# Two more destination blocks summed from gathered rows in a two-layer graph convolution with experts

## What is computed

```python
x = x + gnn(layernorm(x), edges)        # two graph convolutions, each followed by relu
x = x + ffn(layernorm(x))               # top 2 of 8 experts, hidden size 1024, exact gelu

def gcn_conv(x, W, b, src, dst, n):
    h = x @ W
    src_sl, dst_sl = concat(src, arange(n)), concat(dst, arange(n))      # self-loops
    deg = segment_sum(ones_like(dst_sl), dst_sl)
    dinv = rsqrt(deg)
    msgs = h[src_sl] * (dinv[src_sl] * dinv[dst_sl])[:, None]
    return segment_sum(msgs, dst_sl) + b
```

## Time and profile before

| | us |
|---|---|
| runs, three | 2028.27, 2027.53, 2028.29 |
| median | 2028.27 |
| the profiled execution, its own time | 2047.49 |
| its span | 2045.8 |

### The profile page before, as it was taken

The page is one execution under the profiler, slowest core; times in us unless marked ns, Lnnn a source line. Parts: engine busy times, 40 slices in busy tenths (PEclk is TensorE's granted clock), DMA queues, the critical chain, the costliest instruction groups (busy, mean ns, idle before and its releaser), DMA issues. The chain is left out here.

```text
span 2045.8 us, 40624 instructions
## 1 busy us (share of the span) xinstructions
PE 1867.4 (91%) x13425; PEld 1222.5 (60%) x13426; DVE 1345.9 (66%) x3357; ACT 729.1 (36%) x1669; POOL 1146.3 (56%) x1208
## 2 busy tenths in 40 slices
PE   3679999999999998999999999935999999999997
PEld 2545555455555553544444444414989989989996
DVE  6585676676676662566676767567666676666664
ACT  3664444444444440111111111112444444444442
POOL 6215666566676644667666766302566565555553
PEclk8899999999999999999999999965999999999998
DMA  8264455455555437778877887724233322233322
GB/s 282 75 221 167 170 174 188 167 175 191 178 175 175 172 142 269 250 268 269 268 251 266 293 296 255 283 89 179 43 48 50 52 49 45 49 49 48 50 45 27
DMA packets 126408, 329.39 MB, mean 161 GB/s; under 512 B 20736, under 2 KB 80000, under 8 KB 119360
## 3 DMA queue, kind: packets, MB, share of 16 engines
q0 software_dynamic: 59072, 142.05, 26.2%
q1 hardware_dynamic: 47376, 167.36, 22.9%
q10 hardware_dynamic: 19824, 18.23, 2.8%
HBM read 214.10 MB, written 113.45 MB: 160 GB/s over the span
## 5 line engine op out<-in xcount | busy, mean ns | idle before, releaser
L943 PE MATMUL mp_o<-rows,m_counts 128*128 128x512 f16 x1960 | 490.3, 381 | 8.5 <-ACT m_counts L1073 8.5
L585 POOL DMA_INDIRECT m_x_t<-rows_d,take_src x311 | 366.5, 1178 | 204.0 <-PE mp_x L956 155.6
L1889 PE MATMUL rp_o<-rows,adj_ring 128*128 128x512 f16 x1960 | 455.9, 380 | 8.9 <-issue 8.9
L1816 POOL DMA_INDIRECT r_took<-rows_d,take_src x311 | 324.2, 1043 | 178.9 <-PE rp_g L1905 106.2
L1073 ACT ACTIVATE m_counts<-mp 128x490 f16<-128x490 f32 (+4 forms) x544 | 292.1, 559 | 351.9 <-PE mp L972 284.8
L1889 PEld LDWEIGHTS rp_o<-rows,adj_ring 128*128 128x128 f16 x1960 | 191.9, 98 | 225.9 <-issue 11.2
L2447 PE MATMUL fp_h<-f_xt,w 128*128 128x256 f16 x2688 | 305.1, 274 | 0.3 <-issue 0.3
L2466 PE MATMUL fp_y<-w,f_hh 128*128 x2688 | 302.4, 273 | 0.0
L943 PEld LDWEIGHTS mp_o<-rows,m_counts 128*128 128x128 f16 x1960 | 182.8, 98 | 185.2 <-issue 11.6
L2447 PEld LDWEIGHTS fp_h<-f_xt,w 128*128 x2688 | 264.3, 98 | 31.6 <-issue 0.7
L2466 PEld LDWEIGHTS fp_y<-w,f_hh 128*128 128x128 f16 x2688 | 263.0, 98 | 30.4
(11 more groups left out here) (257 smaller groups left out, 1913.0 us busy)
## 6 DMA issues: line engine op xcount, KB each, us to landing
adj<-m_counts SPq DMA_DIRECT2D x40, 1568.0 KB
adj_ring<-adj SPq DMA_DIRECT2D x40, 800.0 KB
adj_ring<-adj SPq DMA_DIRECT2D x40, 768.0 KB
r_raw<-in_L_ffn_W_dram POOLq DMA_DIRECT2D x16, 1024.0 KB
w_parts<-r_parts POOLq DMA_DIRECT2D x8, 1024.0 KB
w<-w_parts SPq DMA_DIRECT2D x4, 2048.0 KB
rows<-in_x_dram SPq DMA_DIRECT2D x7, 896.0 KB, 8.5
rows_d<-rows SPq DMA_DIRECT2D x7, 896.0 KB, 4.7
```

The lines of the kernel that those rows point to most:

```text
L585: pool.indirect_dma_start(out=took[:, r, :], out_offset=None, in_=k.rows_d[0], in_offset=bass.IndirectOffsetOnAxis(ap=k.take_src[:, i:i + ...
L943: mm = nc.tensor.matmul(ps_o[q], counts[:, q, s, :], k.rows[0][:, s, :], start=i == 0, stop=i == BLOCKS - 1)
L1816: pool.indirect_dma_start(out=took[:, r, :], out_offset=None, in_=k.rows_d[1], in_offset=bass.IndirectOffsetOnAxis(ap=k.take_src[:, i:i + ...
L1889: mm = nc.tensor.matmul(ps_o[b % 2], adj[:, m % ADJ_RING, at:at + P], rows[:, s, :], start=s == 0, stop=s == BLOCKS - 1)
```

## The change

DENSE goes from 40 to 38, so TAKEN from 9 to 11 and the TAKES from 311 to 381, in both layers. The banks go from 512 to 487 (4864 destinations are 486.4 banks), and the last of them, which reaches into a taken block, is emptied for the dense block alone. TAKE_END goes from 505 to 480, as the steps of layer one become fewer. To make room, four tables of aims and the layer norm's means and variances move into memory that the count buffers use later, and one small integer tile of layer two into the gates' tile.

```diff
-DENSE = 40
+DENSE = 38
 TAKEN = BLOCKS - DENSE
...
-TAKE_FROM, TAKE_END = 40, 505
+TAKE_FROM, TAKE_END = 40, 480
 TAKE_AT = [TAKE_FROM + i * (TAKE_END - TAKE_FROM) // len(TAKES) for i in range(len(TAKES))]
-BANKS_D = DENSE * P // SPAN
-COLS_D = BANKS_D // P
+BANKS_D = -(-DENSE * P // SPAN)
+COLS_D = -(-BANKS_D // P)
...
-        mv = carve(BLOCKS * 2).bitcast(fp32).rearrange("p (b n) -> p b n", n=2)
...
-        base_i = sb("m_base_i", [P, COLS, BANK_ITEMS], i32)
-        aim = sb("m_aim", [P, COLS, BANK_ITEMS], fp32)
-        aim_end = sb("m_aim_end", [P, COLS, BANK_ITEMS], fp32)
-        aim_neg = sb("m_aim_neg", [P, COLS, BANK_ITEMS], fp32)
...
+        spare = spare[:, SPAN * COLS * COL_BLOCKS:]
+        mv = spare[:, 0:4 * BLOCKS].bitcast(fp32).rearrange("p (b n) -> p b n", n=2)
+        spare = spare[:, 4 * BLOCKS:]
+        base_i, aim, aim_end, aim_neg = (
+            spare[:, 2 * n * COLS * BANK_ITEMS:2 * (n + 1) * COLS * BANK_ITEMS].bitcast(dt).rearrange("p (c j) -> p c j", c=COLS)
+            for n, dt in enumerate((i32, fp32, fp32, fp32)))
...
         def dst_blocks(n):
 
-            return sorted({n * SPAN // P, (n * SPAN + SPAN - 1) // P})
+            return [b for b in sorted({n * SPAN // P, (n * SPAN + SPAN - 1) // P}) if b < DENSE]
...
-        val_i = sb("_val_i", [P, BLOCKS], i32)
...
+        val_i = dense[:].rearrange("p b e -> p (b e)")[:, 0:BLOCKS].bitcast(i32)
```

More of the change, by code:

```diff
@@ L540, in _ @@
         def _(pool):
-            nc.gpsimd.iota(base_i[:], pattern=[[SPAN * P, COLS], [STEP, BANK_ITEMS]], base=0, channel_multiplier=SPAN).then_inc(ids, 1)
+            nc.gpsimd.iota(base_i, pattern=[[SPAN * P, COLS], [STEP, BANK_ITEMS]], base=0, channel_multiplier=SPAN).then_inc(ids, 1)
             nc.gpsimd.iota(ints[:], pattern=[[1, P]], base=0, channel_multiplier=0).then_inc(io_done, 1)
@@ L626, in _ @@
             dve.wait_ge(ids, 1)
-            nc.vector.tensor_scalar(aim_neg[:], base_i[:], -1.0, 0.5, ALU.mult, ALU.add)
+            nc.vector.tensor_scalar(aim_neg, base_i, -1.0, 0.5, ALU.mult, ALU.add)
             nc.vector.memset(limit_neg[:], 0.5 - BLOCKS).then_inc(cells_ready, 1)
-            nc.vector.tensor_scalar(aim_end[:], base_i[:], float(STEP), None, ALU.add)
+            nc.vector.tensor_scalar(aim_end, base_i, float(STEP), None, ALU.add)
             nc.vector.memset(one_h[:], 1.0)
-            link(nc.vector.tensor_copy(aim[:], base_i[:]))
+            link(nc.vector.tensor_copy(aim, base_i))
             dve.wait_ge(heads_in, 16)
@@ L732, in _ @@
             link(nc.vector.tensor_tensor(long[:, 0:COLS * BANK_ITEMS].rearrange("p (c j) -> p c j", j=BANK_ITEMS),
-                                         rows_d[:, :, :, P], aim_end[:], ALU.is_lt))
+                                         rows_d[:, :, :, P], aim_end, ALU.is_lt))
             nc.vector.tensor_reduce(long_any[:], long[:], AX.X, ALU.max).then_inc(long_ready, 1)
@@ L2106, in _ @@
             nc.vector.tensor_scalar(k.pad_value[:], k.token_id[:, BLOCKS - 1:BLOCKS], float(P + 1), None, ALU.add)
-            link(nc.vector.tensor_single_scalar(val_i[:], k.token_id[:], TOP_VALUE - 1, ALU.bitwise_and))
-            link(nc.vector.tensor_scalar(k.value[:], val_i[:], 1.0, None, ALU.add))
+            link(nc.vector.tensor_single_scalar(val_i, k.token_id[:], TOP_VALUE - 1, ALU.bitwise_and))
+            link(nc.vector.tensor_scalar(k.value[:], val_i, 1.0, None, ALU.add))
             nc.vector.memset(eps2[:], EPS * EPS).then_inc(eps_set, 1)
```

## The result

The changed kernel takes 2063.11 us (median of four runs, 2061.41 to 2068.16) against 2028.28 for the kernel before on the same chip: a ratio of 1.0181 with an interval of 1.0163 to 1.0199. It is slower by 34.8 us; the forecast was 6.4 slower. The sign was right and the size was not.

What follows compares the result with a forecast made beforehand. TensorE was taken to set the pace, with GpSimd following within a tenth to a fifth. Layer one -7.4, layer two +13.4 and set-up +0.4 gave +6.4 us on 2028.3: 2034.7 us, range 2010 to 2056.

Steps and rivals of the forecast that it cites:

- pitch term: Layer two: TensorE gains 5.6 us, GpSimd's 1.343 us a gather loses 19 (9.5 in each sixty-slot stretch); +13.4 us.
- rival (d): Layer two: gathers land late behind seven weight stores and loads, up to 6 us each; +19, 2053 us; chance 0.12.
- TensorE's side, layer one: Layer one: 35 blocks take 592.8 us, a gain of 13.4 us if TensorE keeps the pace.
- GpSimd's side, layer one: Layer one: GpSimd needs all the time TensorE's pace allows; 6 us lost, leaving -7.4 us.
- 568 of 568: no margin: Layer one: gathers and self-loop additions need 568 us of GpSimd, and TensorE's 429 steps last 568 us.
- The lead that I charged (6 us): Layer one: one ring lead of about 7 us estimated lost to brief lateness at equal speed, 6 us.
- The rule of the Trainium skill: Layer one: two-input tensor_tensor doesn't hold up GpSimd's descriptor generation, so the full 13.4 us would be gained; the prediction disagreed.
- GpSimd's side, layer two: Layer two: sixty dense slots need 195.7 us of GpSimd against TensorE's 179.2; 9.5 us lost twice, +19.
- The 20 easy slots ... restore the lead: Layer two: between dense stretches GpSimd needs 49.6 of TensorE's 57.1 us and regains its lead.
- (a): Both layers: TensorE keeps the pace, with GpSimd's pitch at 1.25 to 1.27; -18.6, 2009.7 us; chance 0.22.
- (b): Layer two's dense groups at pitch 1.30, 3.5 us lost twice, layer one's gain whole: 2016.7 us; chance 0.12.
- (c): Both layers wait for GpSimd, 5% above mean pitches: layer one +6.6, layer two +34, 2069 us; chance 0.10.

Runs made afterwards that it cites:

- run 1: Changed kernel with every layer-two weight load after the first fetching four columns, stores whole: 2045.09 us, ratio 1.0095.
- run 9: Changed kernel with four-column weight loads after the first, and weight loads and stores issued by ScalarE instead of GpSimd: 2036.59 us, ratio 1.0047.
- run 14: Changed kernel with layer two's gathers after the first eight fetching 64 rows instead of 128, and four-column weight loads after the first: 2043.41 us, ratio 1.0092.
- run 11: Kernel before the change with every layer-two weight load after the first fetching four columns: 2018.19 us, ratio 0.9954.
- run 7: Changed kernel with four-column weight loads after the first and eleven ring slots in layer two instead of eight: 2040.77 us, ratio 1.0066.
- run 2: Changed kernel with layer two's whole weight loads and stores issued by ScalarE instead of GpSimd: 2063.16 us, ratio 1.0177.

## Why the prediction was wrong

Two steps failed, both in layer two. The pitch term ("-5.6 + 19") was too small, since the lead covered less than the 7 us charged and TensorE's own pace was taken as 519 us in place of 509.8. And landings behind the weight transfers, rival (d), stood at nothing in the sum. That GpSimd would set the pace there was right.

**TensorE's side, layer one: right.** 592.8 us was worked out for TensorE's own pace and 594.4 measured.

**GpSimd's side, layer one: right in kind.** "568 of 568: no margin" is the trace after: 5.5 us of slack in all. The lead that I charged (6 us) was lost only to 1.6. The rule of the Trainium skill in "SBUF — State Buffer", Who interferes with whom, priced this layer nearer (-13.4 against -11.9 measured). Its reason isn't borne out: a gather still takes 1.193 us in the mean and 0.942 at least. Of the 381, the 180 beside no one-hot table of VectorE (L821) last 0.950 us in the mean, and each of the 126 above 1.3 us stands beside an m_oh_cell instruction.

**GpSimd's side, layer two: the term that failed.** It stood at 19 us; against TensorE's own pace it measured 37.1 (546.9 with small loads, less 509.8). The mechanism was right: two dense stretches lose, the easy slots between them don't. The sizes were not. Layer two can be cut by dense blocks, five slots to each (us; GpSimd's busy time and slack in brackets; 1, 9 and 14 have small loads):

| slots | after | run 1 | run 9 | run 14 | TensorE alone |
|---|---|---|---|---|---|
| 20 to 79, dense | 190.0 (147.9, 0.2) | 191.2 (148.7, 0.3) | 187.7 (145.6, 0.2) | 184.3 (142.1, 0.8) | 177 |
| 80 to 99, easy | 57.3 (41.8, 3.9) | 56.6 | 59.1 | 57.3 | 57 |
| 100 to 159, dense | 211.8 (152.1, 17.6) | 198.2 (154.6, 1.5) | 190.3 (147.0, 1.4) | 190.8 (146.3, 2.1) | 177 |

The last column is an estimate from run 11: the same sixty slots last 167.1 and 167.4 us there with 107 and 108 gathered matmuls and identities; 37 or 35 more at 0.216 make 175, and one block more is closed. The windows of the dense stretches in after and in run 1, with GpSimd's waits for a free ring slot in the first of after, in its easy slots and in its second (us in total, times, longest; the fixed 0.30 is in them):

```profile
816.31:1006.33 190.02, 179.26 (x830) 87.53 (x829) 119.13 (x442) 27.39 (x57) 147.86 (x145) 0.99 0.79 258
1063.60:1275.40 211.80, 185.37 (x829) 89.65 (x828) 123.07 (x465) 30.17 (x60) 152.13 (x151) 0.94 0.77 257
...
812.93:1004.17 191.24, 180.75 (x830) 87.33 (x828) 119.50 (x442) 27.50 (x57) 148.71 (x146) 0.99 0.73 230
1060.72:1258.95 198.23, 179.71 (x829) 87.11 (x828) 123.41 (x465) 30.16 (x60) 154.60 (x151) 0.99 0.76 248
```

```profile
POOL r_took L1817 <- PE rp_g L1906: 9.0, 29, 0.4
...
POOL r_took L1817 <- PE rp_g L1906: 6.0, 11, 1.6
...
POOL r_took L1817 <- PE rp_g L1906: 27.5, 33, 3.9
```

In after's first stretch none of GpSimd's 138 gaps before gathers is above 0.44 us: its busy time and the fixed gaps (147.9 + 138 x 0.30) are the stretch. Nearly the same holds for both stretches with small loads, and what runs 9 and 14 take off GpSimd's busy time against run 1 (3.1 and 7.6, 6.6 and 8.3 us) comes out of the stretch (3.5 and 7.9, 6.9 and 7.4). Run 14's gathers also move half the bytes, run 9's don't. So GpSimd's pitch sets the dense stretches, but for the whole loads in the second. By its parts:
- GpSimd's need was right: 195.7 us for sixty slots, and 193.3 from gather 35 to gather 175 of after. Its transfers were spread evenly in my sum (7.7 us each); they are 5.2 us of busy time in the first stretch and 9.1 in the second, which has the stores.
- TensorE's pace was not: 519 in place of 509.8, because I took the stage of before as TensorE's own, with its 9.2 us for the loads in it. The row that I used showed one wait of 3.28 us; the 11.4 us of idle time behind the earlier trace rows I didn't break up. In a stretch this is 179.2 in place of about 177.
- The lead was not: 7 us were to cover part of each shortage, and about 3 did in the first (190.0 of a need of 193.3). I took the landing, 3.6 us, from another gather. Layer two's own land 4.5 us after issue in the median and 11.8 at most, and when TensorE waited in the first stretch the gather had been issued 5.4 to 7.1 us before. So with small loads the stretches lost 14 and 21 us, not 9.5 each.
- "The 20 easy slots ... restore the lead" was right: there GpSimd waits for slots again, and the time from a gather's end to its matmul, 8.3 us in the mean for gathers 20 to 29 of after and 5.1 for 170 to 179, is 9.7 for gathers 190 to 209. The lead is back, but TensorE doesn't regain the time that it lost.

Over the whole stage GpSimd's need of 381 x 1.342 + 22.5 = 534 us against 510 is a shortage of 24 that no order of the slots removes; the last 13 us are slack in slots where GpSimd can't run further ahead. Why its mean is 1.03 to 1.04 us with a median of 0.95 is open: in after 39 gathers above 1.1 us hold 23.6 us over the median, as much as the shortage, and no run takes away the work of VectorE beside them.

**Rival (d), left out of the sum.** The loads cost 17.4 us of layer two after and 9.2 before, so the change made them 8.2 dearer (9.0 by the medians: 18.0 and 9.0). The mechanism is as (d) said: a gather behind a store and load lands late. In place of "up to 6 us" seven times, about 2.5 a pair. Most of the 17.4 lies in the second dense stretch (211.8 against 198.2), where GpSimd has 17.6 us of slack in place of 1.5: there it stands still while TensorE waits. (Half of that rival's 42 us is 21, not 19.) The prediction left out what comes after the wait: the granted clock of 0.50. The clock term falls from 12.3 to 2.8 us with small loads and idle time from 41.6 to 30.2. How the 17.4 divide between the two I can't tell, since no run takes the clock away alone.

**Handover.** +4.0 us from layer one's end to the first gathered tile was forecast as nothing. It is there in every run with 38 dense blocks (36.9 to 40.4 us against 33.5 to 34.2 with 39 or 40). In after, 2.63 us of it are one idle stretch of TensorE six matmuls into layer two, put down to "issue"; the reason is open.

**Sum.** -11.9 + 4.0 + (-5.6 + 37.1 + 8.2) - 1.8 = +30.0 us, against 34.8 by the medians. Of the 26.3 us that layer two misses its forecast by, 18.1 are the pitch term (37.1 in place of 19) and 8.2 the landings, which stood at nothing. Some 5 us lie outside these stages or between one profile and a median of runs.

**Rivals (a), (b).** Both needed a pitch of 1.30 or less in layer two; pressed, it is 1.34 in the first dense stretch (1.038 + 0.30). (c), with 2069 us, came nearest in time and for another reason: no gather became slower, layer one held, and layer two lost more than it said.

## What to carry to other kernels

An engine with a third of idle time in the windows can be the next bound. Add the fixed gap between its instructions and sum its need stretch by stretch, as the program's order makes them. Compare that with the other engine's own pace, measured with everything taken out that disturbs it; a stage time that already holds waits flatters the slower side. Take the lead that a ring gives from the landing of the very transfers that use it. Where the need exceeds the pace, a longer ring gains little (run 7). Where it is below, a few more slots are worth having: the kernel before gains 5.7 us by them, and 39 blocks with eleven slots beat both kernels, though how much of that is the 39th block's is not shown.

## What was not expected of the hardware

- An indirect gather of 64 rows occupied GpSimd for 0.900 us (median), one of 128 rows for 0.946. So fewer rows to a gather hardly relieve GpSimd; fewer, larger gathers were not tried.
- A whole weight load without a store cost nothing measurable in either kernel (265.9 against 265.8 us over the first seven after, 248.9 against 248.7 before). Whole loads in place of small ones beside a store of the split weights cost 1.3 us a pair with GpSimd ahead (9.2 over seven) and 2.5 with GpSimd pressed (17.4 over seven); issued by ScalarE they cost no less (layer two 567.9 in run 2 against 542.2 in run 9).
- A wait of 6.43 us cost TensorE more than itself: ten matmuls behind it took 4.47 us in place of 2.32, at a granted clock of 0.50.
